# Attention with fp32 probabilities and values: one plain product in place of a split into fp16 and bf16 parts, in a two-layer transformer kernel on one core

## The reference, cut to what matters

```
scores = jnp.einsum('bhqd,bhkd->bhqk', qr, kr) * scale
scores = jnp.where(padding_mask == 0, jnp.float32(-1000000000.0), scores)
probs = jax.nn.softmax(scores, axis=-1)
out = jnp.einsum('bhqk,bhkd->bhqd', probs, vr)
...
scores = jnp.einsum('bhqd,bhkd->bhqk', q, k) / math.sqrt(DK) + bias
p = jax.nn.softmax(scores, axis=-1)
o = jnp.einsum('bhqk,bhkd->bhqd', p, v)
```

## Time and profile before

| | before |
|---|---|
| median of 3 runs | 988.86 us (988.28 to 990.65) |
| time of the profiled execution | 986.05 us |
| its span in the profile | 984.2 us |
| PE, PEld busy | 772.3, 680.0 us |
| DVE, ACT, POOL busy | 662.2, 614.9, 434.9 us |
| instructions | 19388 |

### The profile page before, as it was taken

One profiled execution on the slowest core, in us unless ns is written; L12 is line 12 of the kernel. 1 busy time (PEld: TensorE's weight loads), 2 busy tenths in 40 slices (PEclk: granted clock), 3 DMA queues, 4 the chain that ended last, 5 costly groups with the idle time before them and its releaser, 6 DMA issues. The chain is left out here.

```text
span 984.2 us, 19388 instructions
## 1 busy us (share of the span) xinstructions
PE 772.3 (78%) x6377; PEld 680.0 (69%) x6377; DVE 662.2 (67%) x2033; ACT 614.9 (62%) x1275; POOL 434.9 (44%) x630
## 2 busy tenths in 40 slices
PE   0567978997897897987988979778432699999995
PEld 0456867886786786776877868766322598888885
DVE  2686888876886985986886777542277366666651
ACT  1485877796687688778679657762000566666662
POOL 5154255253463543454352344133221556666654
PEclk9897898998998998998999988899755799999998
DMA  8698459667368378476565758200040244454432
GB/s 210 151 268 244 112 104 233 168 148 191 92 142 203 111 153 196 116 162 180 122 139 151 182 139 207 64 22 22 27 165 0 55 112 124 129 129 130 129 65 33
DMA packets 100289, 131.13 MB, mean 133 GB/s; under 512 B 8160, under 2 KB 72160, under 8 KB 100192
## 3 DMA queue, kind: packets, MB, share of 16 engines
q1 hardware_dynamic: 94048, 121.52, 48.3%
q0 software_dynamic: 6144, 8.39, 4.9%
HBM read 104.72 MB, written 25.17 MB: 132 GB/s over the span
## 5 line engine op out<-in xcount | busy, mean ns | idle before, releaser
L810 ACT ACTIVATE probs<-neg,neg_max 128x256 f32<-128x256 f32 x512 | 232.7, 506 | 105.9 <-DVE neg_max L659 103.7
L666 DVE TENSOR_TENSOR p_lo<-ps_t,p_hi 128x512 f16<-128x512 f32 x256 | 176.1, 688 | 108.1 <-ACT p_hi L817 108.0
L393 PE MATMUL ps_t<-ident,probs 128*128 128x128 f32 x1024 | 172.4, 295 | 57.9 <-ACT probs L810 57.1
L383 PE MATMUL ps_s<-k_stack,q_stack 128*128 128x256 f32 x512 | 148.7, 375 | 38.4 <-DMA q_stack<-parts_dram 21.1
L393 PEld LDWEIGHTS ps_t<-ident,probs 128*128 128x128 f32 x1024 | 125.0, 150 | 74.3 <-ACT probs L810 73.6
L817 ACT ACTIVATE p_hi<-ps_t 128x512 f16<-128x512 f32 x256 | 150.5, 588 | 32.6 <-PE ps_t L393 31.1
L383 PEld LDWEIGHTS ps_s<-k_stack,q_stack 128*128 128x128 f32 x512 | 95.9, 208 | 55.4 <-issue 30.1
L659 DVE CUSTOM_DVE_ANT_0 neg<-ps_s,bias_t 128x256 f32<-128x256 f32 x256 | 96.6, 414 | 16.4 <-PE ps_s L383 12.7
L1023 POOL TENSOR_TENSOR o_sum<-o_raw 128x128 f32<-128x128 f32 x64 | 30.0, 469 | 169.3 <-ACT o_raw L896 169.3
L1310 DVE TENSOR_TENSOR hid_l<-hid_e,hid_h 128x512 fp32r<-128x512 f32 x64 | 71.0, 1139 | 39.8 <-ACT hid_e L1414 39.8
L659 DVE CUSTOM_DVE_ANT_0 neg<-ps_s,mask_add 128x256 f32<-128x256 f32 x224 | 83.9, 412 | 19.4 <-PE ps_s L383 19.3
(11 more groups left out here) (232 smaller groups left out, 1743.4 us busy)
## 6 DMA issues: line engine op xcount, KB each, us to landing
bias_t<-in_bias SPq DMA_DIRECT2D x64, 512.0 KB, 6.5
k_stack<-parts_dram SPq DMA_DIRECT2D x64, 256.0 KB, 4.2
q_stack<-parts_dram SPq DMA_DIRECT2D x128, 128.0 KB, 4.7
parts_dram<-part_h SPq DMA_DIRECT2D x32, 256.0 KB, 3.2
parts_dram<-part_l SPq DMA_DIRECT2D x32, 256.0 KB, 2.6
w1e<-in_w1e SPq DMA_DIRECT2D x8, 1024.0 KB, 4.8
w2e<-in_w2e SPq DMA_DIRECT2D x8, 1024.0 KB, 5.6
ctxT_A<-in_ctxT SPq DMA_DIRECT2D x8, 256.0 KB, 5.5
```

The source lines that it names most:

```text
L383: ins = nc.tensor.matmul(ps_s[U % 2][:, i * SEQ:(i + 1) * SEQ], q_stack[g % 2][:, h % 2, j, c, qt * P:(qt + 1) * P], k_stack[g % 2][:, j, ...
L393: ins = nc.tensor.matmul(ps_t[U % 2][:, (i * QT + kb) * P:(i * QT + kb + 1) * P], probs[:, U % 2, i, kb * P:(kb + 1) * P], ident[:, :], st ...
L666: nc.vector.tensor_tensor(p_lo[:, U % 4, :], ps_t[U % 2][:, :], p_hi[:, U % 4, :], ALU.subtract).then_inc(lo_ready, 1)
L810: ins = nc.scalar.activation(probs[:, U % 2, i, :], neg[:, U % 4, i, :], ACT.Exp, bias=neg_max[:, U % 4, i:i + 1], scale=-1.0)
```

## The change

The transposed probabilities stay in fp32 and are copied out of `ps_t` once, by DVE for even units and by ACT for odd ones. The values stay in fp32 as well, with the column of ones beside each head's 16 (`VW` = 17), so that `pe_values` has four products for a unit, with 128x128 fp32 stationary and 17 fp32 columns moving. POOL no longer splits anything: it copies the values of A once, and for C ACT writes them straight from PSUM to their place. DVE divides the result straight out of `ps_o` (`ve_o_normalise`), one slot later than DVE's inverse stood; ACT's copy and POOL's three instructions are gone. The load of the next values is issued four slots earlier.

```
-VW = 3 * DK + 1
+VW = DK + 1
...
         def pe_prob_transposes(pe, U):
             pe.wait_ge(exp_ready, U + 1)
-            wait(pe, lo_ready, U - 1)
+            wait(pe, probsT_ready[U % 2], U // 2)
...
-            pe.wait_ge(hi_ready, U + 1)
-            pe.wait_ge(lo_ready, U + 1)
+            pe.wait_ge(probsT_ready[U % 2], U // 2 + 1)
             if u == 0:
-                pe.wait_ge(S["va_ready"] if kind == A else S["vc_ready"], b + 1)
+                pe.wait_ge(S["va_ready"] if kind == A else S["v_copied"], b + 1)
             if u % 4 == 0:
-                wait(pe, o_copied, U // 4 - 1)
+                wait(pe, o_ready, U // 4 - 1)
             for i, h in enumerate(unit_heads(u)):
                 col = h % 8 * VW
-                n = 0
                 for kb in range(QT):
-                    for part in (p_hi, p_lo):
-                        ins = nc.tensor.matmul(ps_o[half][:, col:col + VW],
-                                               part[:, U % 4, (i * QT + kb) * P:(i * QT + kb + 1) * P],
-                                               v_parts[g % 2][:, kb, h, :],
-                                               start=(n == 0), stop=(n == 3))
-                        n += 1
+                    ins = nc.tensor.matmul(ps_o[half][:, col:col + VW],
+                                           probsT[:, U % 4, (i * QT + kb) * P:(i * QT + kb + 1) * P],
+                                           v_ones[g % 2][:, kb, h, :], start=(kb == 0), stop=(kb == QT - 1))
...
-        def ve_low_part(ve, U):
+        def ve_probs_copy(ve, U):
             wait(ve, pv_done, U - 3)
-            ve.wait_ge(hi_ready, U + 1)
-            nc.vector.tensor_tensor(p_lo[:, U % 4, :], ps_t[U % 2][:, :], p_hi[:, U % 4, :],
-                                    ALU.subtract).then_inc(lo_ready, 1)
+            ve.wait_ge(pt_ready, U + 1)
+            nc.vector.tensor_copy(probsT[:, U % 4, :], ps_t[U % 2][:, :]).then_inc(probsT_by_dve, 1)
...
+        def ve_o_normalise(ve, half):
+            g, j = divmod(half, 4)
+            qt, i = divmod(j, 2)
+            heads = ps_o[i][:, 0:8 * VW].rearrange("p (h v) -> p h v", v=VW)
+            ve.wait_ge(pv_done, 4 * half + 4)
+            nc.vector.reciprocal(o_inv[:, i, :, :], heads[:, :, DK:VW]).then_inc(o_inv_ready, 1)
+            ve.wait_ge(o_inv_ready, half + 1)
+            if j == 0 and g > 0:
+                before = SEGMENTS[g - 1]
+                ve.wait_ge(S["oa_T"] if before[0] == A else S["oc_T"], int(before[1]) + 1)
+            dst = attn[:, qt, i * P:(i + 1) * P].rearrange("p (h d) -> p h d", h=8)
+            nc.vector.tensor_tensor(dst, heads[:, :, 0:DK], o_inv[:, i, :, :].to_broadcast([P, 8, DK]),
+                                    ALU.mult).then_inc(o_ready, 1)
...
                     if t + 2 < ALL_UNITS:
                         ve_neg_scores(ve, t + 2)
-                    ve_low_part(ve, t)
                 if half_at(t) is not None:
-                    ve_o_inverse(ve, half_at(t))
+                    ve_o_normalise(ve, half_at(t))
+                if 0 <= t < ALL_UNITS and t % 2 == 0:
+                    ve_probs_copy(ve, t)
...
-        def ac_high_part(ac, U):
+        def ac_probs_copy(ac, U):
             wait(ac, pv_done, U - 3)
             ac.wait_ge(pt_ready, U + 1)
-            nc.scalar.activation(p_hi[:, U % 4, :], ps_t[U % 2][:, :], ACT.Copy).then_inc(hi_ready, 1)
+            nc.scalar.copy(probsT[:, U % 4, :], ps_t[U % 2][:, :]).then_inc(probsT_by_act, 1)
...
                     if t + 1 < ALL_UNITS:
                         ac_exp(ac, t + 1)
-                    ac_high_part(ac, t)
-                if half_at(t) is not None:
-                    ac_o_copy(ac, half_at(t))
+                    if t % 2 == 1:
+                        ac_probs_copy(ac, t)
```

More of the change, by code:

```diff
@@ L30 @@
 BF16 = mybir.dt.bfloat16
-FP16 = mybir.dt.float16
 I32 = mybir.dt.int32
@@ L95, in slots_of @@
         at.update(k=(late + 2, late + 2), k_high=late + 2, k_low=late + 3, xc=late + 5, q=(late + 6, late + 6),
[L96 removed]
+                  q_high=late + 6, q_low=late + 7, v=(late + 8, late + 8), v_copy=late + 8)
     if b > 4:
@@ L169, in build @@
         ctxT = {k: lay(f"ctxT_{k}", [P, DC, SEQ]) for k in (A, C)}
-        v_raw = {k: lay(f"v_raw_{k}", [P, QT, D]) for k in (A, C)}
-        v_rest = lay("v_rest", [P, QT, D])
-        v_parts = [lay(f"v_parts_{k}", [P, QT, H, VW], BF16) for k in range(2)]
+        v_raw = lay("v_raw", [P, QT, D])
+        v_ones = [lay(f"v_ones_{k}", [P, QT, H, VW]) for k in range(2)]
         mask_int = lay("mask_int", [P, QT, SEQ], I32)
@@ L181, in build @@
         probs = lay("probs", [P, 2, 2, SEQ])
[L182 to L185, removed]
+        probsT = lay("probsT", [P, 4, 512])
         attn = lay("attn", [P, QT, D])
@@ L772, in ve_finish @@
                                       ).then_inc(S["logit_ready"], 1)
[L774 to L777, removed]
+        def ve_o_normalise(ve, half):
[11 more added lines that the diff above has]
+                                    ALU.mult).then_inc(o_ready, 1)
         def half_at(t):
-            return (t - 5) // 4 if t >= 5 and t % 4 == 1 and (t - 5) // 4 < ALL_UNITS // 4 else None
+            return (t - 6) // 4 if t >= 6 and t % 4 == 2 and (t - 6) // 4 < ALL_UNITS // 4 else None
         def ve_layers(ve):
@@ L857, in ac_prepare_c @@
                 ac.wait_ge(S["v_out"], b + 1)
-                wait(ac, S["vc_ready"], b)
-                nc.scalar.copy(flat(v_raw[C]), ps_m[1][:, :]).then_inc(S["v_copied"], 1)
+                g = PLACE[C, b]
+                ac.wait_ge(pv_done, (g - 1) * UNITS)
+                nc.scalar.copy(v_ones[g % 2][:, :, :, 0:DK],
+                               ps_m[1][:, :].rearrange("p (t h d) -> p t h d", t=QT, h=H)).then_inc(S["v_copied"], 1)
         def ac_finish(ac, t, b):
@@ L889, in ac_finish @@
                 nc.scalar.copy(flat(nrmT_c), ps_m[1][:, :]).then_inc(S["xr_T_copied"], 1)
[L891 to L896, removed]
         def ac_layers(ac):
@@ L923, in po_rstd @@
             nc.gpsimd.tensor_tensor(rstd[k][:, :], var_eps[k][:, :], half_neg[:, :], ALU.pow).then_inc(ln_rstd[k], 1)
[L925 to L937, removed]
-                    ins = nc.gpsimd.tensor_copy(part[1][:, t], rest[:, t])
-                if n == 3:
-                    ins = nc.gpsimd.tensor_tensor(raw[:, t], rest[:, t], part[1][:, t], ALU.subtract)
-                if n == 4:
-                    ins = nc.gpsimd.tensor_copy(part[2][:, t], raw[:, t])
-            ins.then_inc(step_sem if n < 4 else ready_sem, 1)
         def po_prepare_a(po, t, b):
@@ L964, in po_prepare_a @@
                                         ALU.is_equal, ALU.mult).then_inc(S["mask_ready"], 1)
-            for n in range(5):
-                if t == at["va"] + n:
-                    if n == 0:
-                        po.wait_ge(ld["v_A"], b * 16 + 16)
-                        wait(po, pv_done, max(PLACE[A, b] - 1, 0) * UNITS)
-                    po_split_values(po, A, b, n, S["va_step"], S["va_ready"])
+            if t == at["va"]:
+                po.wait_ge(ld["v_A"], b * 16 + 16)
+                wait(po, pv_done, max(PLACE[A, b] - 1, 0) * UNITS)
+                for n in range(QT):
+                    ins = nc.gpsimd.tensor_copy(v_ones[PLACE[A, b] % 2][:, n, :, 0:DK],
+                                                v_raw[:, n, :].rearrange("p (h d) -> p h d", h=H))
+                ins.then_inc(S["va_ready"], 1)
         def po_rest(po, t, b):
@@ L1568, in prepare_a @@
                     load_mask(b + 1)
-                if t == at["va"] + 5 and b + 1 < NB:
+                if t == at["va"] + 1 and b + 1 < NB:
                     load_va(b + 1)
```

43 lines of the change are left out of this document (8 added, 35 removed).

## The result

The changed kernel takes 1060.62 us (median of 4 runs, 1052.91 to 1070.51), the kernel before in the same series 989.75 us (988.28 to 992.61): the ratio is 1.069, with a 95% interval from 1.065 to 1.072. It is slower by 71 us. The forecast was slower by 186 us, at 1175 us; the measured time lies 6 us under the low end of the range, which was 1067. The profiled execution took 1052.91 us, with a span of 1051.1.

What follows compares the result with a forecast made beforehand. PE was taken as the bound in slots it fills. Its 647 us of stage work over a clock of 0.83, plus 25 us idle, gave 805 us, 186 longer: 1175 us for the kernel, range 1067 to 1290.

Steps and rivals of the forecast that it cites:

- what bounds the kernel: Attention stage: PE fills some slots, where added work goes to the end; in slots with a stall it is hidden.
- the stall of a GELU: PE's idle time of 4.36 us around a GELU shrinks to 3.0 us at full clock.
- The waits costed at nothing: New waits on DVE's division, the copies and the values add nothing; the division 19 us if its cover were gone.
- the relief earns nothing beside the price: Less work on ACT and DVE gains nothing more, as PE's added work fills the same 57.1 us of waits.
- I take 0.83, the middle.: PE's mean clock in the attention stage falls from 0.91 to 0.83, making the stage 805 us, 186 us longer.
- the second rival: The stage's clock stays at 0.91 to 0.97: 78 to 122 us more, chance 0.31.
- a near row for the whole stage: The window 66.0 to 105.6, at clock 0.76, taken as near a stage whose clock falls often.
- PE's work: PE's busy time in the attention stage, at full clock, goes from 470 to 647 us, 177 us more.
- The clock stays as it was: Attention stage at a clock of 0.91 to 0.97: 1067 to 1111 us, chance 0.31.
- A busier PE keeps its clock throughout: Attention stage at a clock of 1.0, 677 us, 58 us more: 1047 us, up to 1067; chance 0.05.
- The clock is held low for long: Attention stage at a mean clock of 0.75 to 0.5: 1248 to 1664 us, chance 0.19.
- Not slower: PE's fp32 weight loads run ahead, a step up to 0.076 us is hidden: 932 to 989 us, chance 0.03.

Runs made afterwards that it cites:

- e1: The kernel before with fp32 products like the changed kernel's, 33 columns, and none of the relief on the other engines: 1078.61 us, ratio 1.083.
- e8: The changed kernel with each fp32 product made twice, 17 columns, sixteen records a unit: 1408.53 us, ratio 1.419.
- e9: The changed kernel widened to 64 columns a head, with each fp32 product made twice: 1206.56 us, ratio 1.220.
- e3: The changed kernel with 64 columns a product in place of 17, 48 of them ones: 1025.05 us, ratio 1.036.
- e6: The changed kernel laid out for 64 columns, streaming 64 in the first five segments and 17 in the eleven others: 1036.96 us, ratio 1.048.
- e4: The changed kernel with probabilities and values as fp32r, one record a product in place of two, 18 columns: 974.93 us, ratio 0.987.
- e5: The changed kernel with 33 columns a head in place of 17: 1051.71 us, ratio 1.065.

## Why the prediction was wrong in its size

**Right: what bounds the kernel.** PE had two sorts of slots, and work added goes to the end in those that it fills. The idle time left was forecast as 25 us and is 23.9; the stall of a GELU as 3.0 us and is 2.75; the wait for the exponential is down to ten cases. That they come so near is in part luck: with the 0.61 us a unit that were really added (see below) the same sum leaves 4.36 - 2 x 0.61 = 3.1 us of a stall, and what took the other 0.4 us was not looked for. The step is 0.112 us, as taken from the router's product, and 17 columns add nothing to it. The waits costed at nothing are nothing: the division takes 292 ns and no copy is among PE's waits. That the relief earns nothing beside the price was too strict: e1 stands 14 us over the changed kernel, by the ratios.

**The step that failed: "I take 0.83, the middle."** The clock in the stage is 0.91, the value that the second rival took. 647 / 0.83 + 25 is 805 us and 647 / 0.91 + 25 is 736: 69 of the 123 us by which the stage was overestimated. What the step rested on is real: e8 and e9 show that PE, busy without a pause, is held low by records that are nearly all weight load, and e3 that this costs the changed kernel some 32 to 36 us, most of it, by e6, in the first five segments. What was wrong is the size. The prediction took as a near row for the whole stage one of a segment with little wide work beside the units, and let it pull the mean down everywhere. In the first five segments its figure is what came: 0.86 before, 0.83 after, with both long spells. In the eleven others, where most slots have a quarter of a layer beside the eight records, the clock was 0.93 and is 0.94: the time at the lower clock did not grow there (61.2 us, then 57.8), though the stretch is 44 us longer. They are 71% of the stage and set its mean. That the wide pieces are what holds the clock there is argued from e3, e6 and e9, in which columns added behind the same loads hold it; no run took the pieces away.

**A term of the sum that was mis-sized: PE's work.** 647 us were forecast, and it is 658.4 x 0.91 = 599. Two parts of the 48 us can be named. The first record's successor starts after 0.031 and not 0.112 us, because the load of the first starts with the last of the transposes, 0.108 us before its product (in the trace at 355.49 and 355.60), where the later ones start 0.028 us before theirs: from the first record to what follows there are 0.81 us in place of 8 x 0.112 = 0.90, and eight records of the old kind took 0.20 us, so a unit got 0.61 us more, 156 us in all and not 177. The other is in how busy time is counted: the record in front of a pause is counted to its end, where in front of other work all but its step overlaps. Before, there were 124 pauses of PE in the stage, and the records right in front of them last 32.2 us in all; after, 19 pauses with 5.5 us. So up to 27 us of the 470 that were carried over as work were ends in front of stalls, and went with these. 21 + 27 is the 48, and at a clock of 0.91 it makes 53 us of the 123; the second part is worked out from the two traces, no run isolates it.

**The rivals.** "The clock stays as it was" is the case that came, with its clock (0.91 to 0.97 was its range). Its 1067 to 1111 us was over the measured time for the work's 48 us, and 6 us of idle time: with 599 in place of 647, and 24 in place of 30, the same sum gives stages of 599 / 0.91 + 24 = 682 and 599 / 0.97 + 24 = 642 us, against 619 before, and so, from 988.86 us, 1052 and 1012. "A busier PE keeps its clock throughout" is wrong here: e8 has PE busy for 99.6% of the stage at a mean clock of 0.77, and only e9, where PE is as busy and streams more, is at 1.00. The page "TensorE: Matmul & The Clock Gate" of the Trainium skill, section "HAM oscillation — how this bites in real kernels", says that the clock stays up while PE is kept busy; e9 agrees with that, and e8 (busy for 88.3 of 88.7 us at 0.50) and the two spells of 30.7 us (busy for 30.5 and 30.7) don't. "The clock is held low for long" happened in two spells, and for nearly half of the stage (485 of 1059 us) only in e8. "Not slower" is right for half the loads (e4), and wrong for the change itself, whose loads start 0.112 us apart: that is the step, and it is over the 0.076 up to which all would have been hidden.

**Open.** Why the gain isn't even over 17, 33 and 64 columns, and why the first long spell is 30.7 us in one execution, 64.9 in e5 and 61.4 in e1, is not settled. Nor is the spread of the times: the changed kernel's four executions go from 1052.91 to 1070.51 us, those of the kernel before from 988.28 to 992.61. The longest has the lowest mean clock, 0.880 against 0.893 in the shortest, but the one of 1061.73 us has 0.892, so the clock does not account for all of it.

## What to carry to other kernels

Count an fp32 product by its weight loads, 0.112 us for each 128x128 one and two to a product, before its columns: where PE is the bound, a split into 16-bit parts, with eight records of 0.025 us, was cheaper than four plain products even with its extra work on the other engines (989 against 1061 us), and fp32r with its four loads was cheaper than either (975). When PE's added work goes into idle time, take the idle time of the filled slots from the timeline, and don't carry the ends in front of stalls over as work. And look at the granted clock where PE is busy all the time: if its records are nearly all weight load, more moving columns can be worth a try: here they cost next to nothing (0.84 us a unit in place of 0.81) and gave 32 to 36 us back. A mean clock for a whole stage is not carried over from one of its segments: take it by segment, with what stands beside the narrow records.

## What the runs showed of the hardware that was not expected

- PE can be busy without a pause at the lower of its two clocks, 1.2 GHz: 88.3 of 88.7 us in e8, with 413 records, of which in a unit without other work 16 of 22 are products with 17 columns behind fp32 loads. It can also fall there: at 135.4, behind 6.9 us with PE busy for 6.9. With 64 columns the same program's stage is at 1.00 throughout (1408.53 against 1206.56 us).
- 64 columns cost what 17 do behind an fp32 load of 128x128: 0.112 us a step in both.
- An fp32r product is one record where an fp32 one is two, at the same 0.112 us (e4: 1024 records in place of 2048); it took the kernel from 1060.62 to 974.93 us.
